# Norm scalars in four batches, group 0's routing inside the last chunk, a tail in steps of two tiles, and GpSimd's first transfers behind a wait

## What is computed

```python
# 1. tokens: patches of 16 time steps (stride 8, edge padded), rfft, times W
xf = jnp.fft.rfft(patches, axis=-2, norm='ortho')
x_emb = jnp.concatenate([x_real, x_imag], axis=-1) @ W.T

# 2. attention of all 8192 tokens with all, then a layer norm
f = _l2norm(feats.reshape(B * N, C))
attn = jax.nn.softmax(jnp.matmul(f, f.T), axis=-1)
feats_fcm = f * 0.8 + jnp.matmul(attn, f) * 0.2
h = _layernorm(h + _l2norm(feats_fcm))

# 3. mixture of 8 experts, top 2, then a layer norm
logits = tokens @ router_w.T            # softmax, top_k 2, renormalised: combine
for e in range(E):
    y = jax.nn.gelu(tokens @ w1[e] + b1[e], approximate=False) @ w2[e] + b2[e]
    out = out + combine[:, e:e + 1] * y
h = _layernorm(h + out)
```

## Time and profile before

| | us |
|---|---|
| median of 3 runs | 940.5 (938.76 to 941.68) |
| the profiled execution | 937.71 |
| its span, first to last instruction | 935.9 |
| PE busy | 878.7 (94%) |
| DVE busy | 765.4 (82%) |
| ACT busy | 650.2 (69%) |
| POOL busy | 145.8 (16%) |
| mean granted clock of TensorE | 0.984 |

### The profile page before, as it was taken

The page is one execution under the profiler, slowest core; times in us unless marked ns, Lnnn a source line. Parts: engine busy times, 40 slices in busy tenths (PEclk is TensorE's granted clock), DMA queues, the critical chain, the costliest instruction groups (busy, mean ns, idle before and its releaser), DMA issues.

```text
span 935.9 us, 30575 instructions
## 1 busy us (share of the span) xinstructions
PE 878.7 (94%) x13276; PEld 438.7 (47%) x13276; DVE 765.4 (82%) x919; ACT 650.2 (69%) x1260; POOL 145.8 (16%) x153
## 2 busy tenths in 40 slices
PE   3998899999999999999999999999999799888885
PEld 2443455555555555555555555555555454333321
DVE  5134988998999899989999988998898788676663
ACT  0134788887888788788887887888787686655543
POOL 3045500000000040000000000000000948432122
PEclk9999999999999999999999999999999999899898
DMA  9797500000000000000000000000000000001001
GB/s 253 197 290 127 98 2 3 2 3 2 2 2 3 3 2 3 2 2 2 3 3 2 3 3 2 3 2 3 2 3 3 2 2 2 1 12 23 12 12 34
DMA packets 28709, 26.52 MB, mean 28 GB/s; under 512 B 9536, under 2 KB 26176, under 8 KB 28576
## 3 DMA queue, kind: packets, MB, share of 16 engines
q1 hardware_dynamic: 19408, 14.98, 7.0%
q10 hardware_dynamic: 8752, 8.93, 3.7%
q0 software_dynamic: 416, 0.66, 0.4%
HBM read 18.28 MB, written 2.10 MB: 22 GB/s over the span
## 4 chain that ended last, share of the span: by engine, by line
PE 84%; DVE 4%; POOL 4%; ACT 3%; DMA 2%; issue 2%; SPq 0%; POOLq 0%; ACTq 0%; DVEq 0%
PE ps L442 33%; PE ps L459 23%; PE ps L472 11%; PE ps L375 6%; PE ps L528 3%; DMA ring<-in_x_dram 2%; PE ps L593 2%; PE ps L485 2%; DVE ring L1003 1%; PE ps L609 1%; ACT ring L772 1%; DVE ring L872 1%; PE ps L506 1%; ACT ring L739 1%; POOL stat L297 1%
## 5 line engine op out<-in xcount | busy, mean ns | idle before, releaser
L872 DVE TENSOR_TENSOR ring<-ring 128x1024 f16<-128x1024 f32 x512 | 602.4, 1225 | 52.2 <-ACT ring L772 50.6
L772 ACT ACTIVATE ring<-ps 128x1024 f32<-128x1024 f32 x512 | 519.3, 1020 | 131.2 <-PE ps L442 130.9
L442 PE MATMUL ps<-big 64*64 64x512 f16 x6144 | 376.8, 377 | 9.4 <-ACT ring L772 9.2
L459 PE MATMUL ps<-ring,fs 64*64 64x512 bf16 x4096 | 274.6, 384 | 0.0
L442 PEld LDWEIGHTS ps<-big 64*64 64x64 f16 x6144 | 171.3, 106 | 173.9 <-ACT ring L772 15.1
L459 PEld LDWEIGHTS ps<-ring,fs 64*64 64x64 f16 x4096 | 116.0, 106 | 110.4 <-issue 0.5
L472 PE MATMUL ps<-ring,fs 64*64 64x512 f16 x2048 | 154.0, 377 | 0.1
L772 ACT ACTIVATION_READ_ACCUMULATOR ring<-ps 128x1 f32 x512 | 101.3, 198 | 0.0
L472 PEld LDWEIGHTS ps<-ring,fs 64*64 64x64 f16 x2048 | 58.5, 107 | 53.5 <-issue 1.2
L739 ACT ACTIVATE ring<-ps,b1s 128x512 f32<-128x512 f32 x64 | 42.1, 683 | 46.8 <-PE ps L528 46.8
L1003 DVE TENSOR_TENSOR ring<-ring,ps 128x512 f32<-128x512 f32 x64 | 43.4, 683 | 33.4 <-ACT ring L739 30.8
(11 more groups left out here) (135 smaller groups left out, 434.9 us busy)
## 6 DMA issues: line engine op xcount, KB each, us to landing
ring<-in_x_dram ACTq DMA_DIRECT2D x8, 1024.0 KB, 15.6
ring<-in_x_dram SPq DMA_DIRECT2D x8, 1024.0 KB, 13.2
big<-big SPq DMA_DIRECT2D x16, 128.0 KB, 2.4
out_dram<-h SPq DMA_DIRECT2D x16, 128.0 KB, 2.4
f<-in_L_tok_W_dram SPq DMA_DIRECT2D x1, 288.0 KB, 4.1
xedge<-in_x_dram POOLq DMA_DIRECT2D x2, 128.0 KB, 9.0
w1s<-in_L_ffn_w_dram POOLq DMA_DIRECT2D x2, 128.0 KB, 8.3
fs<-consts_dram ACTq DMA_DIRECT2D x1, 256.0 KB, 18.8
```

The costliest lines, as they stand in the source:

```text
L442: last = mm(bank(SLOT_BANK[slot_of(s)] + r)[m:m + 64, :], of_k[r][:, 128 * k + m:128 * k + m + 64], of_q[r][:, q0 + 512 * r:q0 + 512 * r + ...
L459: last = mm(bank(sums_bank(s // NT) + half)[m:m + 64, :], fs[64 * r:64 * r + 64, s % NT, m:m + 64], probs[64 * r:64 * r + 64, s % 8, :].bi ...
L772: a(probs[:, s % 8, :], bank(SLOT_BANK[slot_of(s)], 2), ACT.Exp, accum_out=rowsum[:, s:s + 1]).then_inc(s_pr, 1)
L872: tt(probs_lo[:, s % 8, :], probs[:, s % 8, :], probs[:, s % 8, :].bitcast(BF16)[:, 1:2 * QC:2], ALU.subtract).then_inc(s_lo, 1)
```

## The change

Five edits. GpSimd waits for the first tap (`s_weff` 1) before its transfers. The high parts of groups 6 and 7 go from tiles 8 and 12 of attention to tiles 14 and 22. The norm scalars are made in four batches, group 0's alone, with denominators at t = 3, 12 and 21. In the last chunk the jobs of group 0 come earlier, and its gate weights are transposed there too (PE t = 30, ACT t = 31). The tail runs in four steps a group instead of eight half steps: both gelus of a pair one behind the other, both weighings too, with the other jobs of the group between the pairs; ACT no longer waits for the last sums before its first gelu, but before `result_out(0)`.

```diff
-BATCHES = ((0, 2), (2, 5), (5, 8))
-BATCH_AT = (9, 21)
+BATCHES = ((0, 1), (1, 3), (3, 5), (5, 8))
+BATCH_AT = (3, 12, 21)
-LATE_HIGHS = {4: 5, 8: 6, 12: 7}
+LATE_HIGHS = {4: 5, 14: 6, 22: 7}
...
             pool.wait_ge(s_zero, 3)
+            pool.wait_ge(s_weff, 1)
...
                 if q == NQ - 1:
+                    if t == 19:
+                        token_transposes(0)
                     if t == 21:
-                        token_transposes(0)
-                    if t == 23:
                         router_logits(0)
-                    if t == 27:
+                    if t == 29:
                         token_transposes(1)
+                    if t == 30:
+                        combine_transposes(0)
...
             def result_out(z):
                 act.wait_ge(s_dn, 4 * z + 4)
+                if z == 0:
+                    act.wait_ge(s_ph, NC // 2)
+                    act.wait_ge(s_lo, NS)
...
-            act.wait_ge(s_ph, NC // 2)
-            act.wait_ge(s_lo, NS)
-            combine_out(0)
+            act.wait_ge(s_ph, NC // 2 - 1)
+            act.wait_ge(s_lo, NS - 4)
...
+                    if u < NPAIR * NG:
+                        gelu(u, 0)
+                        gelu(u, 1)
+                    if i == 0 and z >= 0:
                         result_out(z)
...
-                    if t == 16:
+                    if t == 14:
                         scaled(0)
-                    if t == 20:
+                    if t == 18:
                         normed(0)
-                    if t == 23:
+                    if t == 25:
                         scaled(1)
+                    if t == 28:
+                        normed(1)
+                    if t == 22:
                         logits_out(0)
...
+                    for step in EARLY_STEPS.get(t, ()):
+                        route(0, step)
...
-            sums_out(NQ - 1)
...
+                    if u < NPAIR * NG:
                         weigh(u, 0)
+                        weigh(u, 1)
+                    if u == 0:
+                        sums_out(NQ - 1)
```

More of the change, by code:

```diff
@@ L611, in result @@
                 last.then_inc(s_y, 1)
-            combine_transposes(0)
             for g in range(NG + 1):
-                for s in range(8):
-                    u = 4 * g + s // 2
-                    if s == 0 and 1 <= g < NG:
-                        combine_transposes(g)
-                    if s % 2 == 0 and 1 <= u < 4 * NG:
+                for i in range(NPAIR):
+                    u = NPAIR * g + i
+                    if 1 <= u < NPAIR * NG:
                         up(u)
-                    if s % 2 == 1 and u < 4 * NG:
+                    if u < NPAIR * NG:
                         expand(u)
-                    if s % 2 == 1 and 1 <= u <= 4 * NG:
+                    if 1 <= u <= NPAIR * NG:
                         down(u - 1)
-                    if g == 0 and s in (0, 2):
-                        sums_tokens(NQ - 1, s // 2)
-                    if s == 1 and g + 1 < NG:
+                    if g == 0 and i < 2:
+                        sums_tokens(NQ - 1, i)
+                    if i == 0 and g + 1 < NG:
                         router_logits(g + 1)
-                    if s == 3 and g >= 1:
+                    if i == 1 and g >= 1:
                         result(g - 1)
-                    if s == 7 and g + 2 < NG:
+                    if i == 2 and g + 2 < NG:
                         token_transposes(g + 2)
+                    if i == 3 and g + 1 < NG:
+                        combine_transposes(g + 1)
         @block.scalar
@@ L1008, in result_added @@
                     ALU.mult, ALU.add).then_inc(s_z, 1)
[L1011 removed]
+            EARLY_STEPS = {22: (0,), 23: (1, 2), 24: (3, 4), 25: (5,), 26: (6, 7, 8), 27: (9, 10, 11), 28: (12,), 29: (13,)}
+            STEPS_OF = ((0, 1, 2), (3, 4, 5, 6, 7), (8, 9, 10, 11, 12, 13), ())
             def beside(q, t):
@@ L1071, in _ @@
                     beside(q, k // 2)
-            sums_out(NQ - 1)
             for g in range(NG + 1):
-                for s in range(8):
-                    u, y, q, z = 4 * g + s // 2, g + 2, g + 1, g - 1
-                    steps = STEPS_OF.get(s, ((), ())) if q < NG else ((), ())
-                    if s % 2 == 1 and u < 4 * NG:
+                for i in range(NPAIR):
+                    u, y, q, z = NPAIR * g + i, g + 2, g + 1, g - 1
+                    if u < NPAIR * NG:
                         weigh(u, 0)
-                    if s % 2 == 0 and 1 <= u <= 4 * NG:
-                        weigh(u - 1, 1)
-                    if g == 0 and s in (1, 3):
-                        sums_crossed(NQ - 1, s // 2)
-                    if g == 0 and s == 4:
+                        weigh(u, 1)
+                    if u == 0:
+                        sums_out(NQ - 1)
+                    if g == 0 and i in (1, 2):
+                        sums_crossed(NQ - 1, i - 1)
+                    if g == 0 and i == 3:
                         sums_variance(NQ - 1)
                         covariance(NQ - 1)
-                        denominators(2)
-                    if s == 2 and q < NG:
+                        denominators(3)
+                    if i == 0 and y < NG:
+                        scaled(y)
+                    if i == 0 and q < NG:
                         logits_out(q)
-                    for step in steps[0]:
-                        route(q, step)
-                    if s == 1 and y < NG:
-                        scaled(y)
-                    if s == 4 and z >= 0:
-                        result_added(z)
-                    for step in steps[1]:
-                        route(q, step)
-                    if s == 6 and z >= 0:
+                    if i == 2 and z >= 0:
+                        result_added(z)
+                    if q < NG:
+                        for step in STEPS_OF[i]:
+                            route(q, step)
+                    if i == 1 and y < NG:
+                        normed(y)
+                    if i == 3 and z >= 0:
                         final_variance(z)
-                    if s == 6 and y < NG:
-                        normed(y)
 _INS = ["x", "L0_tok_W", "L0_ffn_router_w", "L0_ffn_w1", "L0_ffn_b1", "L0_ffn_w2", "L0_ffn_b2"]
```

71 lines of the change are left out of this document (23 added, 48 removed).

## The result

The changed kernel took **906.62 us** (median, 904.54 to 908.16) against 940.08 of the kernel before on the same chip (938.76 to 941.68): ratio 0.9643, 95% interval 0.9628 to 0.9658. Forecast were 904.7 and a range of 896 to 917. The profiled execution took 904.54 us with a span of 902.7 us, 33.2 less than the span before; the sum had said 35.8.

The account below looks back on a forecast made before the run. PE was taken as the bound, busy 878.7 of 935.9 us. Terms 3.7 + 2.8 + 6.5 + 0.7 + 20.9 + 1.2 = 35.8 took the profiled 937.7 to 901.9; the median, 2.8 above, was 904.7 us, range 896 to 917.

Parts of the forecast that it names:

- The start: Loads of x: with GpSimd's transfers moved behind the first tap, PE's awaited load lands sooner; +3.7 us (0 to 4.9).
- Rival (b): Start: GpSimd's transfers only move the congestion, the first term is 0; 908.4 us, chance 0.13.
- High parts: First attention tiles: later high parts of groups 6 and 7 end ScalarE's two waits for f; +2.8 us (1.0 to 3.1).
- Batches and last chunk: Last chunk, step 16: four batches end the wait for norm scalars and its lower clock; +6.5 us (4.8 to 6.5).
- VectorE's lag: Last chunk: denser packing eats VectorE's lead over PE's sums; cost 0 to 1 us, taken 0.
- Junction: From the last scores to group 1: a 2.7 us PE gap remains, lower clock likely; +0.7 us (-0.7 to +3.1).
- Groups 1 to 6: Tail in two-tile steps: every wait is met, a group takes PE's 13.04 us; +20.9 us.
- rival (c): Tail: the waits only change place, 15.9 us a group; 925.6 us, chance 0.08.
- Rival (a): Tail: VectorE bounds it, with routing blocks before weighings, 14.3 us a group; 912.7 us, chance 0.15.
- Group 7 and the end: End of the tail: 24.48 us lose only the wait for yT; +1.2 us.
- Rival (d): Tail: the gap after expand(0) lowers PE's clock for good, about 24 us a group; 971 us, chance 0.04.
- The SBUF rule: First attention tiles: GpSimd's operations cost VectorE 1 us, making the high-parts term 1.8 if VectorE had no lead.

Follow-up runs that it names:

- a_gate_late: Changed kernel with GpSimd's transfers waiting for both halves of the second image instead of the first tap: 905.55 us.
- a_no_gate: Changed kernel with GpSimd's wait for the first tap taken out: 908.18 us.
- a_best: Changed kernel with PE's logits(1) and up(1) before sums_tokens, VectorE's copy before its weighings, GpSimd waiting for image 2, group 0's jobs one step earlier: 896.70 us.
- a_highs_back: Changed kernel with the high parts of groups 6 and 7 back before tiles 8 and 12: 909.46 us.
- b_batches: Kernel before with only the norm scalars in four batches, at steps 3, 12 and 21: 933.32 us.
- a_route_early: Changed kernel with group 0's jobs of the last chunk one step earlier, step 13 and group 1's norm kept in place: 908.33 us.
- a_same: Changed kernel run again unchanged, to show the spread of its stages: 906.68 us.
- b_yt_early: Kernel before with only ScalarE's copy to yT moved right behind the first pair's second gelu: 926.02 us.

## Why the prediction was right, and which terms were off

The span fell by 1.3 + 8.2 + 0.6 + 22.1 + 1.0 = 33.2 us. Most of it, and its place, came out as worked out: the waits that the sum counted on are gone. The total is closer than its terms, though, since start and batches fell short by 3.8 us and the tail brought 1.2 more, and two terms are single draws of stages that vary. Term by term:

- **The start: 3.7 forecast, 1.3 measured (1.7 in the mean).** The mechanism was right, the size not, at two steps. The transfers bit from about 18 us on, close to the 18.7 forecast, but the load wasn't "nearly in" by then: they were in its way, and it came at 21.5 us, not 20.3 (the windows under a_gate_late). And I counted the earlier load in full, without the clock: the first products came so much earlier that PE's wait for the second load grew from 2.2 to 4.3 us, and half clock took 1.2 us back (0.6 in the mean). Rival (b), no gain at all, isn't excluded by a_no_gate alone; the means over twelve executions, and a_gate_late and a_best, speak against it. That the transfers only move the congestion was half true.
- **High parts: 2.8 forecast, 3.1 measured** (a_highs_back), the upper bound; VectorE's lead was enough.
- **Batches and last chunk: 6.5 forecast, 5.1 measured** (8.2 less the 3.1 above). The stall is worth 6.6 (b_batches), so 1.5 was lost. Some 1.1 of it is VectorE's lag, "0 to 1, taken 0": PE's wait before the token transposes of group 1 is 1.47 us instead of the 0.41 of b_batches. The other 0.4 is the step that now holds the gate weights' transposes, 3.08 us against 2.66 (from the scores at 774.58 to those at 777.66; in b_batches from 773.76 to 776.42); my sum had charged 0.3 for them to the junction.

```profile
777.33 0.40 PE L519 MATMUL ps<-ident,comb 128*128 128x128 f16 x4
```

  I had compared the totals of the jobs, 5.3 us against 6.2, where the order counts. Before, group 1's norm, which PE's next transposes need, stood behind routing steps 0 to 4; it now stands behind 0 to 11. From 753.34 to 773.23 us VectorE has no idle time [the rows under a_route_early]: 14 low parts, sixteen jobs, 19.9 us for seven steps in which PE needs 18.4. The row of before that should have warned me is this one of its PE timeline, where the lead was already used up:

```profile
778.68 0.66 PE L497 MATMUL ps<-cst,h 128*128 128x128 f32 x4 [0.18 <-DVE h L930]
```

  The prediction had said that no step of it made PE wait visibly; this row shows 0.18 us. Two experiments failed to win the lag back. That it is the place of the norm behind the routing is argued from these rows; a kernel with the norm ahead of them wasn't tried.
- **Junction: 0.7 forecast, 0.6 measured.** The gap of 2.7 us was 2.59, and the lower clock behind it came, as forecast. That the size came out is luck: a_same, the same kernel, has -3.4 (22.97 against 26.34). Over all executions the old order took 23.5 us in the mean of three, and the new one with the gap of 2.59 us 24.4 in the mean of seven: a loss of 0.9. The bounds, -0.7 to 3.1, were too narrow below, and I had treated the length of the lower clock as a property of the kernel. Nor does the +0.7 follow from the working: 18.18 less 14.7 to 18.2, less 0.3, is -0.3 to +3.2.
- **Groups 1 to 6: 20.9 forecast, 22.1 measured.** The layout held; PE has no wait left in groups 1 to 5, rival (c) falls. (The 4.4 us for the lower clock in two groups are 4.3 by the stages.) The difference is that a group takes 12.77 us, less than the 13.04 that PE had been busy. The instructions are the same; with no gap between them their busy time shrank. That a matmul after a wait shows its full length, and one in a row is overlapped by the next, is my reading and wasn't tested; b_yt_early, with one wait fewer than before, lies between with 12.98. Rival (a) falls too: VectorE is busy 11.1 to 12.2 us a group in groups 1 to 5, and PE doesn't wait for it.
- **Group 7 and the end: 1.2 forecast, 1.0 measured.** b_yt_early has the same 1.0, so it is the copy to yT alone.
- **Rival (d)**, the lower clock through the tail, falls: groups 1 to 6 run at 1.00.

The median came 1.9 us above the forecast, the sum's error of 2.6 less 0.7 by which the distance from profiled execution to median differed.

The SBUF rule from the Trainium skill (SBUF — State Buffer, "Who interferes with whom") can be read off the changed kernel. Groups of VectorE's low parts from 94 to 118 us, where GpSimd is busy 12.35 us, 8.8 of them with operations on f of 128x512, and from 120 to 150 us, where it does nothing:

```profile
L879 DVE TENSOR_TENSOR ring<-ring 128x1024 f16<-128x1024 f32 x18 | 24.2, 1414 | 0.0
...
L879 DVE TENSOR_TENSOR ring<-ring 128x1024 f16<-128x1024 f32 x25 | 29.1, 1217 | 1.9 <-ACT ring L779 1.9
```

A low part takes 0.2 us more beside them. The trace agrees with the rule in direction, but PE stayed busy 23.86 of these 24 us, so it cost nothing, and the 1.8 that the rule would have made of the term is wrong. From 742 to 778 us GpSimd is busy 33.95 of 36 us, with the batches' operations of 16 columns, and a low part takes 1.230 us: beside these small operands it takes 0.01 more than in the stretch where GpSimd does nothing.

## What to carry to other kernels

Where one engine is the bound and the others have room, read its idle time by what ends it, lay the waiting jobs out between its fixed work, and check each wait separately: here one misplaced copy was 12.7 of 33 us. When jobs are packed more densely on a helper engine, don't compare totals: find its last idle moment, and count everything queued between that and the result that the bound engine needs. An expected gap of the matmul engine is worth filling with other work even when it is short: with the gap of 2.59 us gone the junction took 17.86 us instead of 22.40 to 26.34, so beside the gap's own 2.6 us the lower clock behind it cost 1.9 to 5.9 us, a different amount from one execution to the next.
